# One k chunk moved from fp32 to split fp16 in the key-context product, and the last k chunk transposed between two feed-forward passes, in a cross-attention and quantized feed-forward kernel

## The reference

```python
qh = softmax(Wq @ layernorm(x), over the 64 rows of each of 8 heads) * SCALE
kh = softmax(Wk @ c, over the 1024 tokens)
vh = Wv @ c
context = jnp.einsum('bhdn,bhen->bhde', kh, vh)
out = jnp.einsum('bhde,bhdn->bhen', context, qh)
out = jnp.einsum('bcn,oc->bon', out, Wo) + bo[None, :, None]
norm = jnp.maximum(jnp.sqrt(jnp.sum(out * out, axis=1, keepdims=True)), 1e-12)
x = x + out / norm * g * np.sqrt(DIM)
x = x + (layernorm(x) @ w + bias)      # w = (w_int - zp) * scale
```

## Time and profile before

| | |
|---|---|
| median of 3 runs | 634.06 us (633.74 to 636.24) |
| the profiled execution's own time | 635.1 us |
| its span | 633.3 us |
| PE busy | 596.1 us, 94% of the span |
| POOL busy | 548.9 us, 87% |
| DVE busy | 543.2 us, 86% |
| ACT busy | 507.1 us, 80% |
| PE in the chain of waits that ended last | 74% |
| granted PE clock, mean | 0.987 of full speed |

### The profile page before, as it was taken

How to read it: one execution, slowest core, us unless ns; L and a number is a source line. 1 busy time by engine, 2 the same in 40 slices (tenths; PEclk the granted TensorE clock), 3 DMA queues, 4 the chain that set the end, 5 groups by cost and what they waited for, 6 DMA issues and landing times.

```text
span 633.3 us, 10844 instructions
## 1 busy us (share of the span) xinstructions
PE 596.1 (94%) x3431; PEld 380.6 (60%) x3447; DVE 543.2 (86%) x904; ACT 507.1 (80%) x789; POOL 548.9 (87%) x473
## 2 busy tenths in 40 slices
PE   4686799999999999999999999999999999998897
PEld 3454375656657575665657566665756666574654
DVE  4897789898988999888988988898898989889754
ACT  4888789797879879787988979797897978788442
POOL 4268879999999999999999999999899999999630
PEclk9888799999999999999999999999999999999999
DMA  9416658868596876868887885868698595848551
GB/s 324 108 36 147 120 140 152 208 97 208 116 151 184 157 189 129 187 125 171 167 138 184 142 202 117 179 143 141 182 152 198 121 194 116 154 116 162 111 141 67
DMA packets 246969, 96.19 MB, mean 152 GB/s; under 512 B 236136, under 2 KB 237952, under 8 KB 246912
## 3 DMA queue, kind: packets, MB, share of 16 engines
q1 hardware_dynamic: 240576, 72.42, 59.3%
q10 hardware_dynamic: 6336, 23.07, 10.7%
HBM read 28.85 MB, written 8.39 MB: 59 GB/s over the span
## 4 chain that ended last, share of the span: by engine, by line
PE 74%; DVE 9%; ACT 5%; issue 4%; DMA 3%; POOL 3%; SPq 1%; ACTq 0%; POOLq 0%; DVEq 0%
PE ps_m L1619 14%; PE ps_m L1493 7%; PE ps_k L1411 4%; PE ps_o L1503 4%; PE ps_o L1411 4%; PE ps_o L1412 4%; PE ps_o L1413 4%; PE ps_k L1413 4%; PE ps_k L1412 4%; PE ps_q L1411 3%; PE ps_q L1413 3%; PE ps_q L1412 3%; PE ps_ta L1472 2%; PE ps_o L1527 2%; PE ps_tb L1472 2%
## 5 line engine op out<-in xcount | busy, mean ns | idle before, releaser
L514 POOL TENSOR_TENSOR q_tok_lo<-q_exp,q_tok_hi 128x1024 f16<-128x1024 f32 x64 | 135.8, 2132 | 8.1 <-ACT q_tok_hi L748 7.3
L737 ACT ACTIVATE q_exp<-q_exp,w_unit 128x512 f32<-128x512 f32 x128 | 92.9, 726 | 53.4 <-DVE q_exp L1070 53.3
L486 POOL TENSOR_TENSOR q_exp<-q_exp,q_rec 128x1024 f32<-128x1024 f32 x63 | 119.9, 1904 | 4.9
L1065 DVE TENSOR_REDUCE q_nmax<-ps_q 128x8 f32<-128x512 f32 x128 | 86.9, 679 | 28.5 <-PE ps_q L1413 28.2
L1619 PE MATMUL ps_m<-w_int,x_parts 128*128 128x512 f16 x432 | 100.0, 379 | 0.3 <-DMA x_parts<-spare 0.2
L1070 DVE TENSOR_TENSOR q_exp<-ps_q,q_nmax 128x512 f32<-128x512 f32 x128 | 88.5, 692 | 4.4
L522 POOL TENSOR_TENSOR k_lo<-k_exp,k_hi 128x1024 f16<-128x1024 f32 x32 | 82.2, 2569 | 9.2 <-ACT k_hi L678 9.2
L1056 DVE TENSOR_REDUCE k_nmax<-ps_k 128x1 f32<-128x1024 f32 x64 | 77.1, 1205 | 5.2 <-PE ps_k L1413 4.9
L1493 PE MATMUL ps_m<-k_t,c_t 128*128 128x256 f32 x256 | 77.0, 383 | 0.0
L1077 DVE TENSOR_REDUCE q_sum<-q_exp 128x16 f32<-128x1024 f32 x64 | 76.9, 1201 | 0.0
L748 ACT ACTIVATE q_tok_hi<-q_exp 128x1024 f16<-128x1024 f32 x64 | 67.5, 1054 | 7.8 <-POOL q_exp L486 5.4
(11 more groups left out here) (221 smaller groups left out, 1461.7 us busy)
## 6 DMA issues: line engine op xcount, KB each, us to landing
x_res<-in_x ACTq DMA_DIRECT2D x16, 512.0 KB, 3.6
out_x<-y SPq DMA_DIRECT2D x15, 512.0 KB, 2.9
x_in<-in_x ACTq DMA_DIRECT2D x14, 512.0 KB, 4.8
c_in<-in_ctx ACTq DMA_DIRECT2D x14, 512.0 KB, 6.0
x_in<-in_x SPq DMA_DIRECT2D x2, 512.0 KB, 5.6
c_in<-in_ctx SPq DMA_DIRECT2D x2, 512.0 KB, 7.0
q_hi<-q_tok_hi SPq DMA_TRANSPOSE x64, 3.3
q_lo<-q_tok_lo SPq DMA_TRANSPOSE x64, 3.3
```

The costliest lines, as they stand in the source:

```text
L486: nc.gpsimd.tensor_tensor(pair, pair, rec.unsqueeze(2).to_broadcast([P, 2 * HEADS, DH]), ALU.mult).then_inc(qs_done, 1)
L514: nc.gpsimd.tensor_tensor(q_tok_lo[p % 2][:], q_exp[:, 2 * p:2 * p + 2, :].rearrange("p t d -> p (t d)"), q_tok_hi[p % 2][:], ALU.subtract ...
L737: nc.scalar.activation(q_exp[:, j, :], q_exp[:, j, :], ACT.Exp, scale=w_unit[:]).then_inc(qexp_done, 1)
L1065: nc.vector.tensor_reduce(q_nmax[:, j, :], heads, op=ALU.max, axis=AX_X, negate=True).then_inc(qmax_done, 1)
```

## The change

A constant `PARTED = 3` says how many k chunks enter M in fp16. Chunk 2 is now lifted like chunks 0 and 1 (one more small ACT instruction, `k_bias`, ahead of its exponential), still transposed on PE, and split on the way out of PSUM: ACT's `move_tk(0)` and `move_tk(1)` write the fp16 high part to `k_t_hi`, and a new DVE function `low_tk` writes the fp16 rest to `k_t_lo`. `mix_m` has, per token tile, three fp16 matmuls of 384 columns and one fp32 matmul of 128. On PE the order around the feed-forward changes, on DVE `low_tk(0)` and `low_tk(1)` come in before `abs_c`, and `shift_q(5)` and `scale_y(1)` change places.

```diff
+PARTED = 3
-        k_t = sb("k_t", [P, TC, HID - TURNED * P])
+        k_t = sb("k_t", [P, TC, HID - PARTED * P])
...
-                    if j < TURNED:
+                    if j < PARTED:
                         nc.scalar.activation(k_bias[:, j:j + 1], bias, ACT.Identity,
...
+                    to = k_t_hi if TURNED + fc < PARTED else k_t
+                    fc = fc + TURNED if TURNED + fc < PARTED else fc + TURNED - PARTED
+                    nc.scalar.activation(to[:, t0:t0 + 4, fc * P:(fc + 1) * P],
...
+                def low_tk(k):
+                    t0, fc = 4 * (k % 2), TURNED + k // 2
+                    dve.wait_ge(tk_moved, TK * a + k + 1)
+                    if k == 0 and begun(a):
+                        dve.wait_ge(m_ready, a)
+                    part = (slice(None), slice(t0, t0 + 4), slice(fc * P, (fc + 1) * P))
+                    nc.vector.tensor_tensor(k_t_lo[part], (ps_ta, ps_tb)[k % 2][:].rearrange("p (t c) -> p t c", t=4),
+                                            k_t_hi[part], ALU.subtract).then_inc(tklo_done, 1)
...
                     scale_y(0)
+                low_tk(0)
+                low_tk(1)
                 if do_n:
                     abs_c()
                 shift_q(4)
                 invert_k()
                 sum_q(a, 1)
+                shift_q(5)
                 if do_f and i != END:
                     scale_y(1)
-                shift_q(5)
...
-                        three(ps_m[:, 0:TURNED * P], c_t_hi[s][:, t, :], c_t_lo[s][:, t, :], k_t_hi[:, t, :],
+                        three(ps_m[:, 0:PARTED * P], c_t_hi[s][:, t, :], c_t_lo[s][:, t, :], k_t_hi[:, t, :],
                               k_t_lo[:, t, :], start=(t == 0), stop=False)
-                        last = nc.tensor.matmul(ps_m[:, TURNED * P:], c_t[s][:, t, :], k_t[:, t, :], start=False,
+                        last = nc.tensor.matmul(ps_m[:, PARTED * P:], c_t[s][:, t, :], k_t[:, t, :], start=False,
...
                     feed_forward(0, (1,))
+                project_q(4)
+                project_q(5)
+                if do_f and i != END:
+                    feed_forward(1, (0,))
                 transpose_k(2)
-                project_q(4)
                 transpose_k(3)
                 if do_f and i != END:
-                    feed_forward(1, (0, 1))
-                project_q(5)
+                    feed_forward(1, (1,))
```

More of the change, by code:

```diff
@@ L140, in build @@
         k_lift = sb("k_lift", [P, 1])
-        k_bias = sb("k_bias", [P, TURNED])
+        k_bias = sb("k_bias", [P, PARTED])
         k_hi = [sb(f"k_hi{j}", [P, N], F16) for j in range(TURNED)]
         k_lo = [sb(f"k_lo{j}", [P, N], F16) for j in range(TURNED)]
-        k_t_hi = sb("k_t_hi", [P, TC, TURNED * P], F16)
-        k_t_lo = sb("k_t_lo", [P, TC, TURNED * P], F16)
-        k_t = sb("k_t", [P, TC, HID - TURNED * P])
+        k_t_hi = sb("k_t_hi", [P, TC, PARTED * P], F16)
+        k_t_lo = sb("k_t_lo", [P, TC, PARTED * P], F16)
+        k_t = sb("k_t", [P, TC, HID - PARTED * P])
         q_tok_hi = [sb(f"q_tok_hi{r}", [P, 2 * HID], F16) for r in range(2)]
@@ L252, in build @@
         tk_moved = sem("tk_moved")
+        tklo_done = sem("tklo_done")
         tc_ready = sem("tc_ready")
@@ L320, in build @@
         TK = 2 * (HC - TURNED)
+        TS = 2 * (PARTED - TURNED)
         def pipeline(iteration):
@@ L661, in exp_k @@
                                              bias=k_lift[:]).then_inc(kbias_done, 1)
-                        act.wait_ge(kbias_done, TURNED * b + j + 1)
+                        act.wait_ge(kbias_done, PARTED * b + j + 1)
                         bias = k_bias[:, j:j + 1]
@@ L756, in move_tk @@
                         act.wait_ge(m_ready, a)
-                    nc.scalar.activation(k_t[:, t0:t0 + 4, fc * P:(fc + 1) * P],
+                    to = k_t_hi if TURNED + fc < PARTED else k_t
+                    fc = fc + TURNED if TURNED + fc < PARTED else fc + TURNED - PARTED
+                    nc.scalar.activation(to[:, t0:t0 + 4, fc * P:(fc + 1) * P],
                                          (ps_ta, ps_tb)[k % 2][:].rearrange("p (t c) -> p t c", t=4),
@@ L1053, in max_k @@
                         dve.wait_ge(kexp_done, 4 * (b - 1) + j + 1)
-                    if begun(b) and j < TURNED:
-                        dve.wait_ge(kbias_done, TURNED * (b - 1) + j + 1)
+                    if begun(b) and j < PARTED:
+                        dve.wait_ge(kbias_done, PARTED * (b - 1) + j + 1)
                     nc.vector.tensor_reduce(k_nmax[:, j:j + 1], ps_k[:], op=ALU.max, axis=AX_X,
@@ L1293, in iteration @@
                     pick_nibbles(2)
-                    pick_nibbles(3)
+                    low_tk(0)
+                    low_tk(1)
                     shift_q(3)
@@ L1298, in iteration @@
                     set_up_top()
+                    pick_nibbles(3)
                     sum_q(a, 0)
@@ L1469, in transpose_k @@
                         pe.wait_ge(tk_moved, TK * a + k - 1)
+                        pe.wait_ge(tklo_done, TS * a + k - 1)
                     for t in range(4):
@@ L1481, in mix_m @@
                         pe.wait_ge(tk_moved, TK * (a + 1))
+                        pe.wait_ge(tklo_done, TS * (a + 1))
                         pe.wait_ge(tc_moved, 2 * (a + 1))
```

## The result

The changed kernel takes 718.95 us (median of 4 runs, 717.65 to 723.18) against 635.13 us of the kernel before beside it: a ratio of 1.133, 95% interval 1.127 to 1.138. The forecast was 710 us, range 682 to 729; the measured time lies in the range, 9 us above the forecast. The profiled execution took 719.9 us, its span is 718.1 us, 84.8 longer than before.

A forecast was written before the change was run, and what follows sets the result against it. PE bounds the kernel, busy 36.12 of a 36.30 us step. Per full step +3.96 wait, -0.45 M, +2.0 clock = +5.5 us; 13 steps give 71.6, the other steps +4: 710 us, range 682 to 729.

The forecast's parts named there:

- The wait: PE in full steps: project_q(5) waits for shift_q(4), starting 4.61 us after half 0, 3.97 idle; step grows 3.96 us.
- The fall of the clock: PE behind that wait: clock falls to 1.2 GHz in each full step, costing 2.0 us.
- my bounds of 1.7 and 3.4: Price of a clock fall on PE: 1.7 us for a 3.4 us low stretch, 3.4 for 6.8.
- M: PE's M product: a token tile takes 0.71 us instead of 0.76, 0.45 us less per step.
- Two small waits that I had at nothing: Project_k(3) behind the extra k_bias: 0.1 us at most, taken as nothing; no wait of move_m behind exp_k was named.
- growing waits as a sign of being wrong: Full steps: forecast called wrong if a step's other waits grow, for which it saw no reason.
- The sum of a full step: Each of 13 full steps: +3.96 - 0.45 + 2.0 = +5.5 us.
- Steps -1, 0, 1 and 15 and the tail: Outside the full steps: steps 0, 1 and 15 together put at +4 us.
- here or there: Steps 0, 1 and 15: an occasional fall of the clock, included in their +4 us without its own size.

The follow-up runs named there:

- run 2: Kernel before with only PE's new order in full steps, no split and no low_tk: 692.73 us, ratio 1.092.
- run 5: Changed kernel with abs_c moved behind shift_q(4) on DVE, both low_tk still ahead of it: 697.6 us, ratio 1.099.
- run 6: Changed kernel with shift_q(4) right behind scale_y(0) on DVE, low_tk and abs_c behind it: 666.3 us, ratio 1.049.
- run 1: Changed kernel with project_q(5) moved back behind half 1 of the feed-forward in full steps: 644.44 us, ratio 1.014.
- run 4: Changed kernel with 17 added matmuls of 512 columns, result unused, between project_q(4) and project_q(5) in full steps: 692.01 us, ratio 1.090.
- run 3: Changed kernel with PE's old order in full steps, the split kept: 660.81 us, ratio 1.041.
- run 8: Split reordered on DVE and PE against the wait, chunk 2 lifted in move_tk and low_tk without k_bias, step 0's old PE order: 638.08 us, ratio 1.005.
- run 9: As run 8, but chunk 2 split for batches 2 to 14 only, fp32 and old orders in 0, 1 and 15: 634.46 us, ratio 0.999.

## Why the prediction was right, point by point

- **The wait.** Forecast 4.61 us from the end of half 0 to project_q(5), measured 4.59; forecast idle 3.97, in distances 3.95 (the profile writes 3.78, since it counts from the modelled end of the last matmul). It is anchored where I had it: without low_tk in the chain it is on record with 2.59 us (run 2), without abs_c with 2.66 (run 5), without both with 1.51 (run 6), each shorter by the length of what is gone, and moving project_q(5) removed it (run 1).
- **The fall of the clock.** Forecast 2.0 us per step, measured 2.10 by run 4. Of the full steps it came in all 13 of the changed kernel (3.78 us on record, 4.21 in the first), in 12 and 11 of 13 behind 2.59 and 2.66 (runs 2, 5; their first steps 2.66 and 3.09), in one step of run 3 behind 2.14, and in none behind 1.51 to 1.92 (the other steps of run 3, run 6). The length alone doesn't decide it: in step 15 a wait of 2.66 us brought a fall in run 4 and none in the changed kernel. The changed kernel's full steps are of two kinds, as the two windows above show: in eight the clock is 0.96 and they pay 1.5 to 1.7 us, in five it is 0.92 and they pay 2.9. Worked out as in the prediction, that is about 3.3 and 6.9 us at 1.2 GHz. The mean was within my bounds of 1.7 and 3.4; the lower one was set a little too high. That the 2.0 came so near is in part luck: I had picked it between the bounds without knowing how the two kinds would mix. The rule of the Trainium skill (TensorE: Matmul & The Clock Gate, HAM oscillation — how this bites in real kernels), that a kernel whose matmuls wait 3 to 5 us once per tile starts each tile cold, held for the 3.97 us wait. Waits under 3 us, shorter than those of that section's kernel, brought the fall as well in most steps of runs 2 and 5.
- **M.** Forecast 0.45 us less a step, measured 0.43 in PE's instructions (6.11 to 5.68).
- **Two small waits that I had at nothing.** k_bias: mix_out(0) and project_k(3) together take 4.11 us in place of 3.99, so 0.12; in run 8, without this k_bias, a quiet step is 0.13 shorter. Here are its instructions in the changed kernel, the exponential ending at 277.11 + 0.19 = 277.30 and PE's project_k(3) at 277.36:

```profile
275.77 0.29 ACT L663 ACTIVATE k_bias<-k_nmax,k_lift 128x1 f32<-128x1 f32 x1 [0.19 <-DVE k_nmax L1061]
276.10 1.11 ACT L673 ACTIVATE k_exp<-ps_k,k_bias 128x1024 f32<-128x1024 f32 x1
277.11 0.19 ACT L673 ACTIVATION_READ_ACCUMULATOR k_exp<-ps_k,k_bias 128x1 f32 x1
```

  I had written 0.1 at most and taken nothing. And the shorter M ends while ACT is still in exp_k(n, 1), which move_m stands behind:

```profile
269.72 1.11 ACT L673 ACTIVATE k_exp<-ps_k,k_bias 128x1024 f32<-128x1024 f32 x1
270.73 0.20 ACT L673 ACTIVATION_READ_ACCUMULATOR k_exp<-ps_k,k_bias 128x1 f32 x1
270.83 0.68 ACT L786 ACTIVATE m_t<-ps_m,g_fit 128x512 f32<-128x512 f32 x1
```

  M ends at 270.52, ACT takes it at 270.83. In the kernel before, ACT sat idle for 0.20 us until M was there:

```profile
274.92 0.69 ACT L781 ACTIVATE m_t<-ps_m,g_fit 128x512 f32<-128x512 f32 x1 [0.20 <-PE ps_m L1493]
```

  So mix_g comes 1.04 us after M in place of 0.94, and 0.10 of the 0.43 is lost. The kernel before had ACT ready just in time for M, so a shorter M alone meets ACT next. Together the two make 0.22 us a step, 2.9 us in all: I had named growing waits as a sign of being wrong and saw no reason for any.
- **The sum of a full step.** 3.95 - 0.43 + 0.12 + 0.10 + 2.10 = 5.84, measured 5.80, forecast 5.51 (3.96 - 0.45 + 2.0). That is 3.8 us of the 9 that the forecast was short.
- **Steps -1, 0, 1 and 15 and the tail**, the mis-sized term: forecast +4, measured 84.8 - 75.4 = 9.4. Of these 2.9 us stand before the first transpose of the weights, which waited 8.96 us for its DMA in place of 6.08; in the other profiles it was 6.1 to 8.8, so it belongs to the execution and not to the change. The rest, 6.5 where I had 4, is 2.7 up to the first mix_g, 2.3 in step 1, 1.5 from step 15 on, where PE waits 2.66 us for q_exp in place of 1.07. In step 0 I had missed that project_q(5) had moved ahead of set_up_spread, and DVE waits for it:

```profile
40.84 0.29 DVE L1031 TENSOR_REDUCE v_top<-ps_m 128x1 f32<-128x128 f32 x1 [1.77 <-PE ps_m L1424]
```

  Yet putting that order back did not shorten the step, since PE then waited for low_tk (run 8). Leaving the split out did: from project_k(3) of step 0 to mix_g the eight profiles with the split in step 0 take 26.6 to 27.0 us, the three without it (the kernel before, runs 2 and 9) 22.9 to 23.9. So it is the split that costs the 2.7 us there; how they divide between low_tk and what waits behind it is open. In step 1 the clock points to a cause that I had left at "here or there". The two windows, before and changed:

```profile
50.22:93.98 43.76, 36.08 (x187) 22.75 (x187) 34.92 (x58) 35.11 (x53) 35.18 (x29) 0.88 0.63 141
```

```profile
55.77:101.87 46.10, 37.05 (x186) 23.48 (x186) 36.12 (x60) 35.22 (x54) 34.91 (x29) 0.81 0.59 132
```

  With the same split, step 1 of run 1 has the clock at 0.92 and takes 43.36 us. That the 2.3 us are the clock's is likely but not shown, since no run changed step 1 alone.

## What to carry to other kernels

An instruction's cost on an engine with slack is decided by whom it stands in front of: 1.2 us of DVE work in a step with 3.7 to spare became part of a 4.6 us chain, since project_q(5), which waits for the end of that chain, had been moved up to it. When two instructions alternate through a single buffer, write down what stands between them on both engines after the edit. And a wait of TensorE that recurs can have two prices, its length and the slower clock behind it; filling it with useless work tells them apart.

## What the runs showed of the hardware that I had not expected

Behind equal waits the clock falls in one step and not in another: with 2.59 to 2.66 us on record (2.75 as the prediction counts it) 12 of the 13 full steps of run 2 paid about 1.7 us and one paid nothing, with the same instructions. And adding 17 matmuls of 512 columns per step, some 3.8 us of PE work, made the changed kernel 27 us faster.
